# A twelve-layer kernel with three edits: an earlier place for sums of squares, a subtraction on GpSimd, a normalisation on ScalarE

## The reference

```python
# two of the cross sublayers (L0, L3): de-pooling
bidx = cumsum(patch_lens, axis=1) - 1          # 257 end positions a sequence
boundary_mask = zeros((bsz, seqlen)).at[arange(bsz)[:, None], bidx].set(1)
h_patch = rmsnorm(patch_embeds, g_init)         # context row * rsqrt(mean of squares + eps) * g
# ... a decaying scan over h_patch: depool
plug = clip(cumsum(boundary_mask, axis=1) - 1, 0, plen - 1)
return depool[arange(bsz)[:, None], plug] + h

# feed-forward of L0: product keys
sx, ix = top_k(sim[0], 8); sy, iy = top_k(sim[1], 8)    # per token and head, 32 + 32 keys
scores, pk = top_k(sx[..., :, None] + sy[..., None, :], 8)
h = softmax(scores) * gelu_new(x . down_embed[indices])
out = h . up_embed[indices]

# feed-forward of L3: low-rank experts
weights, idx = top_k(softmax(x @ gate_w.T), 2)
out = x @ W_lin.T + b_lin + sum(weights * ((x @ left[idx]) @ right[idx]))
```

## Time and profile before

| | |
|---|---|
| median of 3 runs | 3835.31 us (3830.62 to 3837.56) |
| profiled execution | 3838.41 us, span 3836.6 us, mean granted TensorE clock 0.923 |
| TensorE matmul / weight load | busy 3304.6 us (86%) / 2784.9 us (73%) |
| VectorE | 2641.2 us (69%) |
| ScalarE | 1713.9 us (45%) |
| GpSimd | 1218.1 us (32%) |
| transfers | 255.07 MB, 66 GB/s on average |

### The profile page before, as it was taken

One profiled execution on the slowest core, in us unless ns is written; L12 is line 12 of the kernel. 1 busy time (PEld: TensorE's weight loads), 2 busy tenths in 40 slices (PEclk: granted clock), 3 DMA queues, 4 the chain that ended last, 5 costly groups with the idle time before them and its releaser, 6 DMA issues. The chain is left out here.

```text
span 3836.6 us, 107367 instructions
## 1 busy us (share of the span) xinstructions
PE 3304.6 (86%) x40368; PEld 2784.9 (73%) x40368; DVE 2641.2 (69%) x7693; ACT 1713.9 (45%) x4262; POOL 1218.1 (32%) x1708
## 2 busy tenths in 40 slices
PE   3887899999968888887889999999999999874766
PEld 2675788888846666645779999999989999744345
DVE  6674899999948888756545666556655665469766
ACT  2231677777727777655313333333333333223362
POOL 3552788888813333312300000000000000146032
PEclk8897999999979999988789999999999999968676
DMA  3000000000012222200166566556656666355000
GB/s 94 4 0 36 1 0 0 0 0 0 1 37 72 76 75 76 67 10 6 35 130 128 124 129 130 123 123 129 131 124 128 128 129 129 78 100 82 0 3 25
DMA packets 374911, 255.07 MB, mean 66 GB/s; under 512 B 118484, under 2 KB 371368, under 8 KB 373832
## 3 DMA queue, kind: packets, MB, share of 16 engines
q1 hardware_dynamic: 370248, 246.49, 29.6%
q10 hardware_dynamic: 4352, 4.20, 0.5%
HBM read 234.58 MB, written 15.75 MB: 65 GB/s over the span
## 5 line engine op out<-in xcount | busy, mean ns | idle before, releaser
L2170 ACT ACTIVATE L_xattn_prob<-psum,L_xattn_nmax 128x258 f32<-128x258 f32 x512 | 239.2, 472 | 849.2 <-DVE L_xattn_nmax L2212 849.2
L951 PE MATMUL psum<-L_ffn_share,L_ffn_prob 128*128 128x128 f32 x4096 | 494.2, 278 | 54.8 <-DVE L_ffn_prob L884 54.8
L2304 PE MATMUL psum<-L_xattn_ctxT,L_xattn_q_ctx 128*128 128x257 f32 x2048 | 525.0, 389 | 8.3 <-DMA L_xattn_ctx<-ctx_dram 6.7
L951 PEld LDWEIGHTS psum<-L_ffn_share,L_ffn_prob 128*128 128x128 f32 x4096 | 471.3, 192 | 73.9 <-DVE L_ffn_prob L884 57.2
L769 POOL TENSOR_TENSOR L_ffn_sums<-L_ffn_sims 128x1024 f32<-128x1024 f32 x256 | 486.6, 1913 | 106.6 <-DVE L_ffn_prob L884 106.6
L2333 PEld LDWEIGHTS psum<-L_xattn_probT,L_xattn_ctx 32*128 32x128 f32 x16384 | 469.2, 187 | 50.9 <-DVE L_xattn_q_ctx L2203 45.9
L2333 PE MATMUL psum<-L_xattn_probT,L_xattn_ctx 32*128 32x128 f32 x16384 | 494.0, 273 | 5.9 <-DVE L_xattn_probT L2226 2.1
L2146 POOL TENSOR_TENSOR L_xattn_z_var<-L_xattn_z_mv,L_xattn_z_eps 128x1 f32<-128x1 f32 x32 | 6.1, 191 | 1280.3 <-DVE L_xattn_z_mv L2238 1251.0
L2304 PEld LDWEIGHTS psum<-L_xattn_ctxT,L_xattn_q_ctx 128*128 128x128 f32 x2048 | 361.0, 191 | 64.9 <-issue 11.0
L808 ACT ACTIVATE psum<-L_ffn_sums,L_ffn_bias 128x512 f32<-128x512 f32 x512 | 340.8, 688 | 92.5 <-DVE L_ffn_prob L884 88.7
L884 DVE SCALAR_TENSOR_TENSOR L_ffn_prob<-L_ffn_sums,L_ffn_best,psum 128x512 f32<-128x512 f32 x512 | 357.8, 740 | 5.7 <-ACT psum L808 2.4
(11 more groups left out here) (445 smaller groups left out, 6269.2 us busy)
## 6 DMA issues: line engine op xcount, KB each, us to landing
L_xattn_ctx<-ctx_dram SPq DMA_DIRECT2D x512, 256.0 KB, 5.4
L_xattn_ctxT<-ctx_T_dram SPq DMA_DIRECT2D x128, 257.0 KB, 3.0
L_xattn_k_all<-ctx_T_dram SPq DMA_DIRECT2D x128, 128.5 KB, 2.1
L_xattn_v_all<-ctx_dram SPq DMA_DIRECT2D x128, 128.0 KB, 2.2
L_attn_qkv_scratch<-L_attn_qkv SPq DMA_DIRECT2D x24, 256.0 KB, 2.8
L_attn_rows<-L_attn_qkv_scratch SPq DMA_DIRECT2D x24, 256.0 KB, 5.3
start_raw<-ctx_dram ACTq DMA_DIRECT2D x16, 256.0 KB, 12.3
start_plug_all<-plug_scratch SPq DMA_DIRECT2D x1, 2048.0 KB, 7.2
```

The source lines that it names most:

```text
L951: last = nc.tensor.matmul(pair(2 * s)[:, c * P:(c + 1) * P], prob[:, h % RING, c * P:(c + 1) * P], share[:, h % RING, :], start=(h == 0 an ...
L2170: ins = nc.scalar.activation(prob[:, s, g, :], scores(s)[:, g, :], ACT.Exp, bias=nmax[:, s, g:g + 1], accum_out=total[:, s, g:g + 1])
L2304: last = nc.tensor.matmul(scores(s)[:, g, 0:CTX], q_ctx[:, p, c, b, h:h + 4, :].rearrange("p h n -> p (h n)"), ctxT[:, b, c, :], start=(c ...
```

## The change

In `start`, VectorE's four reductions and L309 move ahead of the wait for plug_all, and the eight copies of PSUM into `depool` go from VectorE to the end of ScalarE's program. In `product_key_experts` the subtraction of `bests` goes to GpSimd, as `differences`: for tile t+1 it stands behind GpSimd's third sum of that tile, and at the very start ahead of the first sum; a new semaphore, `bested`, tells of the eight maxima. VectorE keeps the bias, and add_to_x moves from after head 5 to after head 7. In `lora_experts` the normalisation goes from VectorE (subtract mean, multiply) to ScalarE (scale and bias in one activation), and GpSimd makes the bias, minus mean times the power, in two more small instructions; moments(g+2) and GpSimd's power for g+2 now wait until group g is normalised.

```diff
@@ start @@
+            for q in range(TILES * P // 512):            # block.scalar, at its end
+                act.wait_ge(scanned, q + 1)
+                nc.scalar.copy(core.depool[:, q * 4:q * 4 + 4, :],
+                               core.psum[:, q, :].rearrange("p (t s) -> p t s", s=P)).then_inc(mat_done, 1)
...
-            dve.wait_ge(plug_in, 16)                       # block.vector
-            then_wait(nc.vector.tensor_scalar(plug_all[:, :], plug_all[:, :], rowpos[:, :], None, ALU.is_equal))
-            nc.vector.tensor_tensor(pick[:, :, :, :], ...).then_inc(pick_done, 1)
             for q in range(LOADS):
                 dve.wait_ge(squared, q + 1)
...
             nc.vector.tensor_scalar(ms[:, 1, :], ms[:, 0, :], 1.0 / CD, LN_EPS, ALU.mult, ALU.add).then_inc(summed, 1)
-            for q in range(TILES * P // 512):
-                dve.wait_ge(scanned, q + 1)
-                nc.vector.tensor_copy(core.depool[:, q * 4:q * 4 + 4, :], ...).then_inc(mat_done, 1)
+            dve.wait_ge(plug_in, 16)
+            then_wait(nc.vector.tensor_scalar(plug_all[:, :], plug_all[:, :], rowpos[:, :], None, ALU.is_equal))
+            nc.vector.tensor_tensor(pick[:, :, :, :], ...).then_inc(pick_done, 1)
@@ product_key_experts @@
+            def differences(t, s):                         # block.gpsimd
+                pool.wait_ge(bested, t + 1)
+                nc.gpsimd.tensor_tensor(shift[:, :, :], best[:, s, :, :], best[:, s, :, 0:1].to_broadcast([P, H, TOP]),
+                                        ALU.subtract).then_inc(cut, 1)
...
                     nc.gpsimd.tensor_tensor(sums[:, h % RING, :, :], sx, sy, ALU.add).then_inc(summed, 1)
+                    if h == 2 and before:
+                        differences(t, s)
...
             pair_sums(0, 0)
+            differences(0, 0)
...
                 for h in range(H):                         # block.vector, bests
-                    nc.vector.max(best[:, s, h, :], pairs[:, h, :])
-                dve.drain()
-                nc.vector.tensor_tensor(shift[:, :, :], best[:, s, :, :],
-                                        best[:, s, :, 0:1].to_broadcast([P, H, TOP]), ALU.subtract).then_inc(cut, 1)
+                    last = nc.vector.max(best[:, s, h, :], pairs[:, h, :])
+                last.then_inc(bested, 1)
+                dve.drain()
                 nc.vector.tensor_scalar(bias[:, s, :], ..., -1.0, None, ALU.mult).then_inc(biased, 1)
...
-                    if before and h == 5:
+                    if before and h == 7:
                         dve.wait_ge(out_done, t)
                         add_to_x(core, t - 1, OUT)
@@ lora_experts @@
+            def normal_factors(g, v):                      # block.gpsimd
+                lo, hi = v * S, (v + 1) * S
+                front.pool_rstd(pool, g * S - v * S, only=slots(v))
+                pool.drain()
+                nc.gpsimd.tensor_tensor(shifted_mean[:, lo:hi, 0:1], front.mv[:, lo:hi, 0:1], front.rstd[:, lo:hi, :], ALU.mult)
+                pool.drain()
+                nc.gpsimd.tensor_scalar(shifted_mean[:, lo:hi, 1:2], shifted_mean[:, lo:hi, 0:1], -1.0, None,
+                                        ALU.mult).then_inc(centred, 1)
...
                 if live(-2):
-                    front.pool_rstd(pool, g * S + 2 * S - v * S, only=slots(v))
+                    pool.wait_ge(front.normed, (g + 1) * S)
+                    normal_factors(g + 2, v)
...
+            def normalise(g, v, waits):                    # block.scalar
+                act.wait_ge(centred, g + 1)
+                if waits:
+                    act.wait_ge(front.turned, (g - 1) * S)
+                for s in slots(v):
+                    nc.scalar.activation(front.xn[:, s, :], core.x[:, g * S + s - v * S, :], ACT.Identity,
+                                         bias=shifted_mean[:, s, 1:2], scale=front.rstd[:, s, :]).then_inc(front.normed, 1)
...
                 if live(0):
                     exp(g)
+                if live(0) and live(-2):
+                    normalise(g + 2, v, True)
...
+            normalise(0, 0, False)
+            normalise(1, 1, False)
             groups(-1, 1, step)
...
                 if live(-2):                               # block.vector
+                    dve.wait_ge(front.normed, (g + 1) * S)
                     moments(g + 2, v)
                 if live(0):
                     weigh(g, v)
-                if live(-2):
-                    normalise(g + 2, v, True)
```

More of the change, by code:

```diff
@@ L294, in _ @@
                                                          rowpos[:, :], ALU.mult, ALU.add))
-            dve.wait_ge(plug_in, 16)
-            then_wait(nc.vector.tensor_scalar(plug_all[:, :], plug_all[:, :], rowpos[:, :], None, ALU.is_equal))
-            nc.vector.tensor_tensor(
-                pick[:, :, :, :], plug_all[:, :].rearrange("p (t b s) -> p t b s", t=TILES, b=BT),
-                core.c("group").rearrange("p (a b c) -> p a b c", a=1, c=1).to_broadcast([P, TILES, BT, SEQ]),
-                ALU.mult).then_inc(pick_done, 1)
             part = TILES // LOADS
@@ L309, in _ @@
             nc.vector.tensor_scalar(ms[:, 1, :], ms[:, 0, :], 1.0 / CD, LN_EPS, ALU.mult, ALU.add).then_inc(summed, 1)
-            for q in range(TILES * P // 512):
-                dve.wait_ge(scanned, q + 1)
-                nc.vector.tensor_copy(core.depool[:, q * 4:q * 4 + 4, :],
-                                      core.psum[:, q, :].rearrange("p (t s) -> p t s", s=P)).then_inc(mat_done, 1)
+            dve.wait_ge(plug_in, 16)
+            then_wait(nc.vector.tensor_scalar(plug_all[:, :], plug_all[:, :], rowpos[:, :], None, ALU.is_equal))
+            nc.vector.tensor_tensor(
+                pick[:, :, :, :], plug_all[:, :].rearrange("p (t b s) -> p t b s", t=TILES, b=BT),
+                core.c("group").rearrange("p (a b c) -> p a b c", a=1, c=1).to_broadcast([P, TILES, BT, SEQ]),
+                ALU.mult).then_inc(pick_done, 1)
             dve.wait_ge(rs_done, 1)
@@ L729, in product_key_experts @@
         front = Front(core, outer, f"{name}2", S, lambda s: core.psum[:, 7, 0:P])
-        (centred, simmed, sims_ready, topped, paired, valued, squared, cubed, tanhed, gelued, cut, exped, inverted, shared, biased, summed, probs, used, kept,
+        (centred, simmed, sims_ready, topped, paired, valued, squared, cubed, tanhed, gelued, bested, cut, exped, inverted, shared, biased, summed, probs, used, kept,
          mixed, out_done) = (core.sem(f"{name}_{n}") for n in (
-             "centred", "simmed", "sims_ready", "topped", "paired", "valued", "squared", "cubed", "tanhed", "gelued", "cut", "exped", "inverted", "shared", "biased", "summed", "probs", "used",
+             "centred", "simmed", "sims_ready", "topped", "paired", "valued", "squared", "cubed", "tanhed", "gelued", "bested", "cut", "exped", "inverted", "shared", "biased", "summed", "probs", "used",
              "kept", "mixed", "out_done"))
@@ L3110, in lora_experts @@
         xnT = sb("xnT", [D, 3, S, P])
-        (zeroed, w_in, biased, xnT_done, gated, shifted, exped, weighted, turned, narrowT_done, out_done, added, stored) = (core.sem(f"{name}_{n}") for n in (
-            "zeroed", "w_in", "biased", "xnT_done", "gated", "shifted", "exped", "weighted", "turned", "narrowT_done", "out_done", "added", "stored"))
+        shifted_mean = sb("shifted_mean", [P, 2 * S, 2])
+        (zeroed, w_in, centred, biased, xnT_done, gated, shifted, exped, weighted, turned, narrowT_done, out_done, added, stored) = (core.sem(f"{name}_{n}") for n in (
+            "zeroed", "w_in", "centred", "biased", "xnT_done", "gated", "shifted", "exped", "weighted", "turned", "narrowT_done", "out_done", "added", "stored"))
         block = st.enter_context(nc.Block())
@@ L3143, in _ @@
             nc.gpsimd.memset(right[:, :, :], 0.0).then_inc(zeroed, 1)
-            front.pool_rstd(pool, 0, only=slots(0))
-            front.pool_rstd(pool, 0, only=slots(1))
+            normal_factors(0, 0)
+            normal_factors(1, 1)
             pool.wait_ge(w_in, 16 * (3 + S))
@@ L3179, in moments @@
                 front.dve_moments(dve, g * S - v * S, only=slots(v))
[L3181 to L3184, removed]
             def choose(g, v):
@@ L3241, in _ @@
             moments(1, 1)
-            normalise(0, 0, False)
-            normalise(1, 1, False)
             groups(0, 1, step)
```

## The result

The changed kernel takes 3809.05 us (median of 5 runs, 3800.43 to 3813.73), the one before 3836.33 in the same session (5 runs, 3830.62 to 3841.24): a ratio of 0.9921, 95% interval 0.9904 to 0.9937 (the ratio is estimated together with its interval; the quotient of the two medians is 0.9929). So it is faster, by a little under 1%. 3810.1 was forecast, 25.2 less than before; the two medians differ by 27.3. The profiled execution has a span of 3808.8 us and a granted clock of 0.925; before it was 3836.6 and 0.923.

What follows compares the result with a forecast made beforehand. Time is a sum of stages on one core, with VectorE's waits setting the touched ones. Savings 8.5 + 10.5 + 1.7 + 4.5 = 25.2 take 3838.4 to 3813.2; runs' median 3.1 lower: 3810.1 us, range 3783 to 3822.

Steps and rivals of the forecast that it cites:

- First stage: First stage: reductions fill VectorE's 14.21 us hole and ScalarE copies PSUM; next stage starts at 55.2, 8.5 us less.
- The loop: Product-key stage: moved addition and GpSimd subtraction save 0.35 us a tile, 10.5 us over 30 tiles.
- first rival: Product-key stage: the bias gets through instead of waiting for GpSimd's sum; 1.14 us a tile, kernel 3786 us; 12%.
- The case of 0.01 ahead: Product-key stage, first tile: L851 came at 416.10, GpSimd's sum at 416.11, and L851 still took 2.00 us.
- The start of that stage: Start of the product-key stage: GpSimd begins its sums only after the first maxima; 1.7 us less, bounds 0 and 2.4.
- the first product waits for one sum: Start of product-key stage: first product waits 1.91 us for one sum, not 3.77 for two; about 1.9 earlier.
- three sums still to do that were done before: Start of product-key stage: GpSimd work left over, set against about 1.9 us gained; 1.7 taken.
- Last stage: Last stage: normalisation moves to ScalarE, shortening VectorE's step from 7.71 to 5.5 us; 4.5 us less, between 0 and 10.
- the higher level: Last stage: with TensorE's clock at its higher level, each of five full steps gains 2.2 us, 11 in all.
- the lower level: Last stage: at TensorE's clock of 0.50, a step takes about 6.5 to 7 us; five gain 0.7 each, 3.5.
- rival 3: Product-key stage: GpSimd's subtraction is late and the reduction stalls; at 2.3 us the kernel takes 3846, slower; 4%.
- the break-even: Product-key stage: GpSimd's subtraction time at which a tile costs 21.12 us as before, put at 1.45; cover ends at 1.2.

Runs made afterwards that it cites:

- experiment 3: Four kernels from the changed one: bias made by GpSimd, 3777.99 us; by a two-input VectorE instruction, 3811.95; by a VectorE reduction, 3785.85; GpSimd drain before its third sum, 3790.17.

## Why the prediction was right

- *First stage*: forecast 8.5, measured 8.9 (63.6 to 54.7); over all profiles the next stage starts at 63.0 in the mean of five with the old order and at 54.1 of nine with the new. The last ScalarE copy ended at 54.43, forecast 54.85. The data of the fourth square came at 29.4, not at 28.5, and the last reduction ended at 33.66, not 32.7: free, since the positions came at 36.86. The comparison beside GpSimd's power was taken at no loss, and had none.
- *The loop*: forecast 20.77 a tile, measured 20.76, and from the first weigh to the last 10.7 against 10.5. Each step of it stands in the trace: no wait before L173 in the steady loop, subtraction 0.29, the first need of GpSimd's memory in the very hundredths in which the third sum starts, and lost there. The choice between forecast and first rival, 0.36 or 1.14 a tile, hung on that, and experiment 3 shows both branches: held with two kinds of instruction, and free with a third kind, on another engine or with a pause. The prediction had the bias due 0.01 us ahead of the sum; in the trace it is recorded 0.02 us behind it. The case of 0.01 ahead that it argued from is that of the kernel with the addition moved alone: there the subtraction is recorded within 0.01 us of the sum's start, and is held in all 27 tiles. The rival's sums were right as well: 19.89 to 20.17 where it had near 20.0.
- *The start of that stage*: forecast 1.7, and this term failed. From GpSimd's pair sums to the first weigh it takes 32.25 in the profile of before, but 30.1, 30.4 and 30.0 in the three other profiles with the old order, and 30.1, 31.0, 31.0 and 31.0 in four with the new one: no gain in the mean. The step that failed is what the prediction set against "the first product waits for one sum". That product does come earlier (6.6 to 8.0 us behind the pair sums instead of 8.1 to 10.0), but "three sums still to do that were done before" was priced at 0.2 us. From the first product to the first weigh the changed kernel takes 23.5 us, the one before 22.3: VectorE waits 2.2 us between the products of the first tile instead of 1.4, and 1.10 before the reduction instead of 0, which is more than the shorter bias gives (1.16, where subtraction and bias took 2.1).
- *Last stage*: forecast 4.5 out of 0 to 10, measured 6.6 and, alone, 7.1. At the start 1.6 are given back, where 2 were forecast (first gate copy at 9.91 instead of 8.33); the seven steps give 7.2 and the end 0.9. The term that was mis-sized is the price of a step. The two steps at a clock of 1.00 gained 2.0 and 2.5, near the 2.2 forecast for the higher level. At the lower level the forecast took 6.5 to 7 us a step, a gain of 0.7; the three steps at 0.55 or 0.56 took 7.5 to 7.8 and gained -0.1, 0.2 and 0.9. The first step gave 2.3 more, and the last took 0.5 back. So the forecast's total came close with a wrong price for the slow steps and with steps that it had not counted.
- The sum of the touched terms, 8.9 + 10.7 + 0 + 6.6 = 26.2, lies about a microsecond from forecast (25.2) and result (27.3). Two misses of 1.7 and 2.1 in opposite directions helped, and that was luck. The whole kernel's time could not have told them: its interval, 0.9904 to 0.9937, spans 24 to 37 us.
- In rival 3 the break-even is a slip: a cover of 1.2 and a gain of 0.35 give 1.55 us, not 1.45, so its 3846 should be 3843. It changes no chance, and the subtraction took 0.29.

## What to carry over

When a wait is taken out, work out what the next instruction will meet: here two waits of 1.16 and 0.98 us a tile were removed and 0.36 came back, since everything behind them moved into the next lock. Where VectorE must work beside a busy GpSimd, choose reductions, maxima or instructions with a PSUM operand (beside a sum a reduction took 0.22 us here, a maximum 0.21, a product 0.74, none of them held); and where one must be of the held kind, put a short GpSimd instruction that waits for the same event in that place, so that no long one is running: that was worth four times the edit itself in this loop.

## What was unexpected of the hardware

Back-to-back GpSimd instructions leave nothing between them for VectorE: a tensor_scalar that came 0.02 us before the end of one sum waited 1.92 us, over all of the next, in each of the steady tiles; 0.23 us between the sums were enough for it to pass (0.17 us). The page of the Trainium skill named above speaks of whichever is issued first. The rows can't say which of the two that was, since the next sum is itself recorded 0.04 us before the last one ends and the bias 0.02 us behind its start; they show that an instruction that comes in those last hundredths does not get in ahead of the next sum.

Not every GpSimd instruction holds VectorE. The power of the first stage (L252) runs from 34.43 to 39.89, and the comparison (L309, a tensor_scalar, the bias's kind) started inside it and took 2.35 us, as it does without a power beside it. The masking behind it (L310), with two inputs in SBUF, began 0.6 us before the power's end and took 4.42, the same as before. Had either waited for the power's end as the bias waits for a sum's, it would have been longer by 3.0 or 0.6 us. What sets the power apart from the sums is open; the starts and ends of GpSimd's records are rough, but 3 us is far beyond that.
